# Relative values in an attention kernel: table parts side by side, both probability parts in one matmul, mask on GpSimd

## The chip, the core and the metric

The kernel runs on one core of a Trainium2 chip. The metric is the device time of one execution in microseconds; the median of the runs shown counts. TensorE is PE in the rows of the profile (its weight loads PEld), VectorE is DVE, ScalarE is ACT, GpSimd is POOL, and SyncE, which issues the DMAs, is SP. On-chip memory is SBUF; PSUM is the memory that matmuls write to.

## The reference

Two batches of 2048 tokens with 256 features go through a layer norm, then through attention with relative positions and through a mixture of experts (8 experts, top 2), which are added to the input. The attention has 16 heads of 16 features each, so there are 32 (batch, head) pairs of 2048 x 2048 scores:

```python
rel_pos = jnp.arange(L)[None, :] - jnp.arange(L)[:, None] + (MAX_LEN - 1)
rel_k = relative_k[rel_pos]          # indices outside the 511 rows wrap or clamp
rel_v = relative_v[rel_pos]
scores = jnp.einsum('bhld,bhrd->bhlr', Q, K) * scale
scores = scores + jnp.einsum('bhld,lrd->bhlr', Q, rel_k)
attn = jax.nn.softmax(scores, axis=-1)
out = jnp.einsum('bhlr,bhrd->bhld', attn, V)
out = out + jnp.einsum('bhlr,lrd->bhld', attn, rel_v)
```

The change is in the last line, the relative values: for query row l and key row r the row `rel_v[l, r]` depends on r - l alone. Far from the diagonal it is a constant row, which the kernel adds to V. Near the diagonal (9 key blocks of 128 around each query block of 128, offsets -6 to 2) it is worked out from a table.

## The kernel before

The program has three stages, one after the other: `project` (layer norm, projections, router), the attention stage, and `mix` (experts and output). The change touches a little of the first and the middle one.

**Units and steps.** A unit is one query block of 128 rows (16 per head, `NB`) of one of the 32 heads, so 512 units. The attention stage is a software pipeline over k = 0, 1, 2, ...: in step k each engine works at several units that lie some steps apart (`LAG_S`, `LAG_A`, `LAG_X`, `LAG_PV` are 3, 4, 5 and 6). The order of instructions on each engine is the order of the code in its `step` function; there is no planner. Eight units are a half head (`HALF_C`).

**What a step does.** PE multiplies queries and keys into the score banks (L918), turns the scores so that keys lie on partitions (L952 and L960), and multiplies probabilities and values (L984). DVE reads each score bank once for the maximum (L1146 and L1150, `search_bank`). ACT takes the exponentials of four banks into `pt_full` (L1077). Each of the four becomes a high part in 16 bits (a cast: `high_part`, two on DVE at L1170, two on ACT at L1085) and a low part, the difference to the full number (a subtraction: `low_part`, three on GpSimd at L850, the fourth on DVE at L1178). High parts are cast first, since the low parts read them; GpSimd's first low part of a unit waits for DVE's first cast of it. On DVE a step runs: sums and masks of the relative values if there are any, searches of banks 0 and 2, the fourth low part of the unit before, the two casts, searches of banks 1 and 3, the maximum.

**Relative values.** The parts of the probabilities near the diagonal stay in `pt_near[half]` (part, unit of the half head, offset, query). For a half head `rel_values` (L1011) runs through 16 groups a of 8 neighbouring queries (`SHIFTS` is 8). The stationary operand is a window of 128 columns of the table, in which partition p holds the rows of `rel_v` shifted by p; its 128 columns are 8 shifts of 16 features. The moving operand is 64 columns, 8 units by 8 queries, so every query meets all 8 shifts although only one is its own. Table and probabilities are each split in a high and a low part, and three matmuls are made per offset: high table with high probabilities, high table with low ones, low table with high ones. This makes 16 x 9 x 3 = 432 matmuls for a half head, 54 in a step. Eight groups fill the one PSUM bank `r_ps`; DVE then multiplies the bank by the 0/1 mask of the right shifts into `rel_out` in SBUF (`mask_values`, L1203, twice in a half head), and PE waits for this before it fills the bank again. Afterwards PE turns `rel_out` (`pick_values`, L1026) and DVE sums over the shifts (`sum_values`, L1211). GpSimd adds this to the values' part and scales it (`output`, L861 and L864).

**GpSimd's other work.** In four steps of each head (k % 16 from 7 to 10) it also prepares the values of the next head (`v_part`, L835 to L839), two instructions a step.

## Time and profile before

| | |
|---|---|
| Median of 3 runs | 3461.26 us (3460.48 to 3466.33) |
| Span of the profiled execution | 3463.7 us, 165,894 instructions |
| PE busy over the span | 3194.2 us (92%) |
| DVE | 2813.3 us (81%) |
| ACT | 2634.6 us (76%) |
| POOL | 2262.5 us (65%) |
| Granted TensorE clock, mean | 0.953 of full speed |

For the profiled execution the page gives its span, from the first to the last instruction, and no time of its own beside it; the span is 2.4 us above the median of the runs. The attention stage takes about 2700 us of it. Busy time of an engine is the union of its instructions; a matmul's entry includes its latency, so that PE can count as busy while it could take more work. Neighbouring entries on DVE and POOL overlap a little for the same reason.

### The profile page before, as it was taken

To read this page: it belongs to the slowest core of one execution; us is meant where nothing else is said; L and a number is where in the kernel's file an instruction comes from. 1 tells how busy PE (TensorE), PEld (TensorE's weight loads), DVE (VectorE), ACT (ScalarE), POOL (GpSimd) and SP (SyncE) were. 2 spreads that over 40 slices of the span, in tenths; PEclk is the share of its full clock that TensorE was granted. 3 is DMA by queue.
4 is the path that set the end of the run, shared out by engine and by line. 5 is a ranking of instruction groups with operands and counts; after the bars stand their busy time and mean duration, and the time that the engine had idled before them with its cause. 6 is when DMAs were issued, how large, how long until landed. Compare 5 with 4: busy or idle time off the path is not lost. (4 is left out here: it accounts for less than half of the span.)

```text
span 3463.7 us, 165894 instructions
## 1 busy us (share of the span) xinstructions
PE 3194.2 (92%) x64918; PEld 2524.8 (73%) x64918; DVE 2813.3 (81%) x7853; ACT 2634.6 (76%) x5852; POOL 2262.5 (65%) x2526
## 2 busy tenths in 40 slices
PE   7589999999999999999999999999999996999990
PEld 4357777777777777777777777777777785579980
DVE  6479999999999999999999999999999986534443
ACT  3288888888888888888888888888888893234440
POOL 0167777777777777777777777777777774700006
PEclk9779999999999999999999999999999997589995
DMA  7776666666666666666666666666666664712224
GB/s 212 228 230 216 221 220 221 221 221 224 218 221 224 221 223 224 222 218 224 221 223 224 223 217 221 224 224 221 224 218 222 222 217 161 239 51 69 62 62 145
DMA packets 356374, 701.28 MB, mean 202 GB/s; under 512 B 59545, under 2 KB 168706, under 8 KB 355346
## 3 DMA queue, kind: packets, MB, share of 16 engines
q1 hardware_dynamic: 349458, 673.92, 60.3%
q0 software_dynamic: 6144, 16.79, 1.5%
q8 instruction: 518, 8.49, 1.1%
q14 instruction: 254, 2.08, 0.2%
HBM read 343.02 MB, written 347.46 MB: 199 GB/s over the span
## 5 line engine op out<-in xcount | busy, mean ns | idle before, releaser
L850 POOL TENSOR_TENSOR pt_near<-pt_full,pt_near 128x512 f16<-128x512 f32 (+3 forms) x1984 | 1857.7, 965 | 583.8 <-DVE pt_near L1170 583.8
L1077 ACT ACTIVATE pt_full<-pb,exp_bias 128x512 f32<-128x512 f32 x2048 | 1313.5, 688 | 305.7 <-PE pb L960 183.9
L1011 PEld LDWEIGHTS pb<-pt_near,table_high 128*128 128x128 f16 x18432 | 794.6, 97 | 145.1 <-issue 106.4
L1011 PE MATMUL pb<-pt_near,table_high 128*128 128x64 f16 (+6 forms) x18432 | 884.8, 187 | 15.7 <-DVE rel_out L1203 14.6
L1150 DVE TENSOR_REDUCE part_max<-pb 128x1 f32<-128x512 f32 (+3 forms) x1376 | 771.2, 574 | 131.0 <-PE pb L918 130.0
L1011 PE MATMUL pb<-pt_near,table_low 128*128 128x64 f16 (+6 forms) x9216 | 851.4, 187 | 0.0
L1011 PEld LDWEIGHTS pb<-pt_near,table_low 128*128 128x128 f16 x9216 | 772.7, 97 | 0.0
L1146 DVE CUSTOM_DVE_ANT_0 near_sum<-pb,skewed 128x512 bf16<-128x512 f32 (+3 forms) x1216 | 675.6, 571 | 109.4 <-PE pb L918 85.0
L952 PE MATMUL pb<-ident,skewed 128*128 128x128 f32 x3840 | 621.6, 285 | 20.5 <-ACT q_max L1101 19.2
L1170 DVE CAST pt_near<-pt_full 128x512 f16<-128x512 f32 (+3 forms) x1280 | 532.3, 466 | 0.3 <-PE pb L984 0.3
L984 PE MATMUL pb<-v_head,pt_near 128*128 128x33 f16 x13440 | 507.2, 178 | 9.1 <-POOL pt_near L850 5.5
L984 PEld LDWEIGHTS pb<-v_head,pt_near 128*128 128x128 f16 x13440 | 431.6, 96 | 48.3 <-POOL pt_near L850 31.0
L1069 ACT COPY rel<-pb 128x384 f32<-128x384 f32 x1024 | 437.6, 486 | 37.2 <-PE pb L901 32.4
L952 PEld LDWEIGHTS pb<-ident,skewed 128*128 128x128 f32 x3840 | 409.0, 141 | 49.0 <-ACT q_max L1101 32.2
L1085 ACT CAST pt_near<-pt_full 128x512 f16<-128x512 f32 (+3 forms) x896 | 426.5, 527 | 0.0
L918 PE MATMUL pb<-k_stack,q_stack 48*128 48x512 f16 (+3 forms) x2592 | 402.0, 336 | 24.3 <-DVE part_max L1146 18.0
L960 PE MATMUL pb<-q_max,k_stack 50*128 50x128 f16 x8192 | 409.8, 220 | 15.6 <-ACT pt_full L1077 13.6
L960 PEld LDWEIGHTS pb<-q_max,k_stack 50*128 50x128 f16 x8192 | 232.5, 95 | 183.9 <-issue 137.9
L1479 POOL DMA_INDIRECT stage<-y_slots_scratch,slot x64 | 60.6, 947 | 366.4 <-DMA y_slots_scratch<-y_group 347.2
L1178 DVE TENSOR_TENSOR pt_far<-pt_full,pt_far 128x512 f16<-128x512 f32 (+3 forms) x416 | 293.8, 706 | 0.0
L1085 ACT CAST pt_far<-pt_full 128x512 f16<-128x512 f32 (+3 forms) x416 | 247.0, 594 | 0.0
L901 PE MATMUL pb<-rk_stack,q_stack 48*128 48x384 f16 x1024 | 179.9, 326 | 39.2 <-DMA q_stack<-planes_scratch 30.5
(182 smaller groups left out, 4063.3 us busy)
## 6 DMA issues: line engine op xcount, KB each, us to landing
skewed<-rel_scratch SPq DMA_DIRECT2D x256, 576.0 KB, 5.3
rel_scratch<-rel SPq DMA_DIRECT2D x416, 319.5 KB, 3.4
rel_scratch<-rel SPq DMA_DIRECT2D x320, 320.0 KB, 2.8
skewed<-rel_scratch SPq DMA_DIRECT2D x64, 512.0 KB, 4.6
skewed<-rel_scratch SPq DMA_DIRECT2D x64, 448.0 KB, 4.3
k_stack<-planes_scratch SPq DMA_DIRECT2D x192, 96.0 KB, 4.7
planes_scratch<-planes SPq DMA_DIRECT2D x64, 256.0 KB, 2.3
rel_scratch<-rel SPq DMA_DIRECT2D x64, 256.0 KB, 2.7
```

The source lines that it names most:

```text
L850: ins = nc.gpsimd.tensor_tensor(pt_piece(c, 1, a, z, near), pt_full[e][:, (a - 4 * g) * P:(z - 4 * g) * P], pt_piece(c, 0, a, z, near), AL ...
L918: ins = nc.tensor.matmul(ps[:, a - bank * CH:z - bank * CH], q_stack[b][tile_rows(tile), c * P:(c + 1) * P], k_stack[b][tile_rows(tile), k ...
L952: nc.tensor.matmul(x_ps[e % 2][:, (blk - 4 * g) * P:(blk - 4 * g + 1) * P], skewed[u % 4][:, col:col + P], keep["ident"][:, :], is_transpo ...
L960: ins = nc.tensor.matmul(x_ps[e % 2][:, i * P:(i + 1) * P], k_stack[b][tile_rows(tile, STACK + 2), kind_of(c, blk), col:col + P], q_max[u ...
L984: ins = nc.tensor.matmul(o_ps[:, i * VW:(i + 1) * VW], src[:, cols], rhs, start=(blk == 0 and part == 0), stop=(blk == NB - 1 and part == 1))
L1011: ins = nc.tensor.matmul(acc[:, c0:c1, :], keep[table][:, w:w + P], pt_near[half][:, part, c0:c1, d - M_LO, a * SHIFTS:(a + 1) * SHIFTS], ...
L1069: nc.scalar.copy(rel[k % 2][:, n * half:(n + 1) * half], bank_of("rel", k, n)[:, 0:half]).then_inc(s_ge, 1)
L1077: nc.scalar.activation(pt_full[e][:, :], x_ps[e % 2][:, :], ACT.Exp, bias=exp_bias[:, 0:1]).then_inc(s_exp, 1)
L1085: ins = nc.scalar.copy(pt_piece(c, 0, a, z, near), pt_full[e][:, (a - 4 * g) * P:(z - 4 * g) * P])
L1146: ins = nc.vector.tensor_tensor_reduce(out=near_sum[:, col:col + z - a], in0=src, in1=skewed[k % 4][:, col:col + z - a], scale=1.0, scalar ...
L1150: ins = nc.vector.tensor_reduce(best, src, axis=AX.X, op=ALU.max)
L1170: ins = nc.vector.tensor_copy(pt_piece(c, 0, a, z, near), pt_full[e][:, (a - 4 * g) * P:(z - 4 * g) * P])
```

## The change

The table's high and low part now lie side by side, 16 features of the one and 16 of the other, so that a window of 128 columns holds 4 shifts of both. `SHIFTS` falls to 4 and the groups of queries rise to 32. The moving operand holds both parts of the probabilities, 2 x 8 units x 4 queries = 64 columns, in runs of 4 neighbouring elements where there were 8. One matmul then makes all four products (the low table with the low probabilities was not made before). A half head takes 32 x 9 = 288 matmuls, 36 in a step.

The two halves of the bank (high and low probabilities) must be added. DVE does this as it reads the bank: a reduction over pairs into a new SBUF buffer `rel_raw` (`read_values`). The bank now fills four times in a half head, so there are four such reads where there were two masks. The mask moves to GpSimd, which reads `rel_raw` and writes `rel_out` (`mask_values`, two in a half head, each 16 groups x 8 units x 4 queries, 512 elements per partition). The transposes come one step later (`LAG_SEL`), and so do the sums on DVE and the output on GpSimd. In the first stage the table is written to memory and read back in two DMAs instead of four, with the same bytes.

```diff
-SHIFTS = P // DK
+PLANES = 2
+SHIFTS = P // (PLANES * DK)
+COPIES = PLANES * SHIFTS
...
-LAG_SEL = LAG_RV + HALF_C
+LAG_SEL = LAG_RV + HALF_C + 1
...
+FILLS = 4
+FILL_A = SHIFT_GROUPS // FILLS
...
+            def mask_values(it, h, part):
...
+                pool.wait_ge(s_rle, FILLS * h + (part + 1) * FILLS // 2)
+                if part == 0 and h:
+                    pool.wait_ge(s_sel, PICK_BANKS * h)
+                half_a = SHIFT_GROUPS // 2
+                rows = slice(part * half_a, (part + 1) * half_a)
+                dst = rel_out[:, :, rows, :].rearrange("p c a b -> p a c b")
+                src = rel_raw[:, rows, :].rearrange("p a (c b) -> p a c b", c=HALF_C)
+                mask = keep["shift_mask"][:, :].rearrange("p (x y b) -> p x y b", x=1, y=1)
+                nc.gpsimd.tensor_tensor(dst, src, mask.to_broadcast([P, half_a, HALF_C, SHIFTS]), ALU.mult).then_inc(s_rlm, 1)
...
                 if exists(it, u):
                     for e in range(E - 1):
                         low_part(it, u, e)
+                for part in range(2):
+                    h, j = half_at(k, LAG_RV + (part + 1) * (HALF_C // 2))
+                    if j == 0 and h >= 0 and exists(it, h * HALF_C):
+                        mask_values(it, h, part)
...
-                a = 2 * j + quarter // 2
-                ds = range(M_LO, M_HI + 1)
-                order = (0, 1, -1, -2, 2, -3, -4, -5, -6)
-                order = order[:5] if quarter % 2 == 0 else order[5:]
...
-                    w = table_window(d, a) * DK
-                    for n, (table, part) in enumerate((("table_high", 0), ("table_high", 1), ("table_low", 0))):
-                        ins = nc.tensor.matmul(
-                            acc[:, c0:c1, :], keep[table][:, w:w + P],
-                            pt_near[half][:, part, c0:c1, d - M_LO, a * SHIFTS:(a + 1) * SHIFTS],
...
+                    w = table_window(d, a) * PLANES * DK
+                    ins = nc.tensor.matmul(
+                        acc[:, :, c0:c1, :], keep["table"][:, w:w + P],
+                        pt_near[half][:, :, c0:c1, d - M_LO, a * SHIFTS:(a + 1) * SHIFTS],
...
+            def read_values(it, h, n):
...
+                dve.wait_ge(s_rl, FILLS * h + n + 1)
+                if n % 2 == 0 and h:
+                    dve.wait_ge(s_rlm, 2 * (h - 1) + n // 2 + 1)
+                src = r_ps[:, :].rearrange("p (a q m) -> p a m q", a=FILL_A, q=PLANES)
+                nc.vector.tensor_reduce(rel_raw[:, n * FILL_A:(n + 1) * FILL_A, :], src, axis=AX.X,
+                                        op=ALU.add).then_inc(s_rle, 1)
...
-                h, j = half_at(k, LAG_RV + 4)
-                if j == 0 and h >= 0 and exists(it, h * HALF_C):
-                    mask_values(it, h, 0)
-                h, j = half_at(k, LAG_RV + 8)
-                if j == 0 and h >= 0 and exists(it, h * HALF_C):
-                    mask_values(it, h, 1)
+                for n in range(FILLS):
+                    h, j = half_at(k, LAG_RV + (n + 1) * (HALF_C // FILLS))
+                    if j == 0 and h >= 0 and exists(it, h * HALF_C):
+                        read_values(it, h, n)
```

How the order moves is seen at three places. The first is GpSimd, in the four steps of a head that also hold value work; this is the order before, in which L850 are low parts, L861 and L864 the output, and L835 to L839 the value work:

```order
75 L850 TENSOR_TENSOR pt_near<-pt_full,pt_near 128x384
76 L861 TENSOR_TENSOR out<-rel_sum,o_sum 128x128
77 L864 TENSOR_TENSOR out<-out,inv_sum 128x128
78 L837 CAST v_head<-v_in 128x16x16
79 L839 TENSOR_TENSOR v_head<-v_in,v_head 128x16x16
80 L850 TENSOR_TENSOR pt_near<-pt_full,pt_near 128x512 x2
81 L850 TENSOR_TENSOR pt_near<-pt_full,pt_near 128x256 x2
82 L835 TENSOR_TENSOR v_full<-v_in,rv_lo 128x256
83 L837 CAST v_head<-v_full 128x16x16
```

The same place of the changed kernel, where L856 are the low parts, L872 is the mask, and L880 and L883 are the output:

```order
78 L856 TENSOR_TENSOR pt_near<-pt_full,pt_near 128x384
79 L843 CAST v_head<-v_in 128x16x16
80 L845 TENSOR_TENSOR v_head<-v_in,v_head 128x16x16
81 L856 TENSOR_TENSOR pt_near<-pt_full,pt_near 128x512 x2
82 L856 TENSOR_TENSOR pt_near<-pt_full,pt_near 128x256 x2
83 L880 TENSOR_TENSOR out<-rel_sum,o_sum 128x128
84 L883 TENSOR_TENSOR out<-out,inv_sum 128x128
85 L841 TENSOR_TENSOR v_full<-v_in,rv_lo 128x256
86 L843 CAST v_head<-v_full 128x16x16
87 L856 TENSOR_TENSOR pt_near<-pt_full,pt_near 128x512 x2
88 L856 TENSOR_TENSOR pt_near<-pt_full,pt_near 128x384
89 L856 TENSOR_TENSOR pt_near<-pt_full,pt_near 128x128
90 L872 TENSOR_TENSOR rel_out<-rel_raw,shift_mask 128x16x8x4
```

The output stands one step later, and a mask follows the low parts of a step, ahead of the value work; it stands so in four steps of each head (k % 16 of 1, 5, 9 and 13), three of which have no value work.

The second is DVE at the step in which the sums stand. Before, the two sums (L1211) and the read of the values' bank (L1189, L1190) follow the maximum (L1160, L1162) and precede the next searches:

```order
347 L1160 TENSOR_REDUCE neg_max<-part_max 128x1
348 L1162 TENSOR_REDUCE max_parts<-part_max 128x2
349 L1211 TENSOR_REDUCE rel_sum<-pb 128x64 x2
350 L1189 RECIPROCAL inv_sum<-pb 128x8
351 L1190 TENSOR_REDUCE o_sum<-pb 128x128
352 L1146 ISA near_sum,part_max<-pb,skewed 128x512
```

In the changed kernel a read of the relative values' bank (L1220) stands behind the sums (L1229):

```order
361 L1180 TENSOR_REDUCE neg_max<-part_max 128x1
362 L1182 TENSOR_REDUCE max_parts<-part_max 128x2
363 L1229 TENSOR_REDUCE rel_sum<-pb 128x64 x2
364 L1220 TENSOR_REDUCE rel_raw<-pb 128x256
365 L1166 ISA near_sum,part_max<-pb,skewed 128x512
```

The read of the values' bank has stayed in its step, and is now one step ahead of the sums; the other three reads of a half head stand two, four and six steps behind, each alone at the start of its step.

The third is PE, one group a of the relative values. Before, it is 27 matmuls, of which the first 9 are:

```order
220 L1011 MATMUL pb<-pt_near,table_high 128x64 x2
221 L1011 MATMUL pb<-pt_near,table_low 128x64
222 L1011 MATMUL pb<-pt_near,table_high 128x64 x2
223 L1011 MATMUL pb<-pt_near,table_low 128x64
224 L1011 MATMUL pb<-pt_near,table_high 128x56 x2
225 L1011 MATMUL pb<-pt_near,table_low 128x56
```

In the changed kernel it is 9:

```order
216 L1031 MATMUL pb<-pt_near,table_pairs 128x64 x2
217 L1031 MATMUL pb<-pt_near,table_pairs 128x2x28
218 L1031 MATMUL pb<-pt_near,table_pairs 128x2x24
219 L1031 MATMUL pb<-pt_near,table_pairs 128x64
220 L1031 MATMUL pb<-pt_near,table_pairs 128x2x20
221 L1031 MATMUL pb<-pt_near,table_pairs 128x2x16
222 L1031 MATMUL pb<-pt_near,table_pairs 128x2x12
223 L1031 MATMUL pb<-pt_near,table_pairs 128x2x8
```

A step holds four such groups where it held two of the old ones; the numbers of columns are the same.

## Rows read from the trace of the kernel before

**Rows 1.** The view by cores: span and mean granted clock.

```profile
core 0: 3463.7 us, clock 0.953
```

**Rows 2.** Busy time by stretch (from:to, length, each engine with its instructions).

```profile
1000.00:2000.00 1000.00, 969.18 (x22698) 771.60 (x22692) 911.55 (x2631) 888.31 (x2009) 780.45 (x879) 1.00 0.68 221
```

**Rows 3.** ACT's groups by form, 1000 to 2000 us: count | busy, mean ns.

```profile
L1091 ACT ACTIVATE max_parts<-max_parts,neg_max 128x2 bf16<-128x2 bf16 x190 | 57.2, 301 | 0.0
```

**Rows 4.** The waits, 1000 to 2000 us: total us, times, longest.

```profile
POOL pt_near L850 <- DVE pt_near L1170: 210.9, 154, 2.7
ACT pt_full L1077 <- PE pb L960: 63.8, 118, 1.4
...
DVE part_max L1150 <- PE pb L918: 47.1, 72, 1.5
...
DVE near_sum L1146 <- PE pb L918: 30.2, 48, 1.0
```

**Rows 5.** The timeline of POOL, 1440 to 1530 us: start, length, [idle before].

```profile
1458.22 3.44 POOL L850 TENSOR_TENSOR pt_near<-pt_full,pt_near 128x512 f16<-128x512 f32 x3 [2.36 <-DVE pt_near L1170]
...
1501.75 3.59 POOL L850 TENSOR_TENSOR pt_near<-pt_full,pt_near 128x384 f16<-128x384 f32 x4 [2.14 <-DVE pt_near L1170]
1506.61 3.45 POOL L850 TENSOR_TENSOR pt_near<-pt_full,pt_near 128x512 f16<-128x512 f32 x3 [1.27 <-DVE pt_near L1170]
...
1511.90 3.60 POOL L850 TENSOR_TENSOR pt_near<-pt_full,pt_near 128x512 f16<-128x512 f32 x4 [0.90 <-DVE pt_near L1170]
```

**Rows 6.** The timeline of DVE in a step without extra work.

```profile
1504.23 0.69 DVE L1150 TENSOR_REDUCE part_max<-pb 128x1 f32<-128x512 f32 x1 [0.66 <-PE pb L918]
...
1505.44 0.69 DVE L1178 TENSOR_TENSOR pt_far<-pt_full,pt_far 128x512 f16<-128x512 f32 x1
1506.05 0.76 DVE L1170 CAST pt_near<-pt_full 128x512 f16<-128x512 f32 x2
```

**Rows 7.** The timeline of POOL in a step with value work.

```profile
1482.59 1.16 POOL L850 TENSOR_TENSOR pt_near<-pt_full,pt_near 128x512 f16<-128x512 f32 x1
1483.69 0.88 POOL L837 CAST v_head<-v_full 128x256 f16<-128x256 f32 x1
1484.72 0.68 POOL L839 TENSOR_TENSOR v_head<-v_full,v_head 128x256 f16<-128x256 f32 x1
1485.35 1.16 POOL L850 TENSOR_TENSOR pt_near<-pt_full,pt_near 128x512 f16<-128x512 f32 x1
```

**Rows 8.** The timeline of DVE in the same step.

```profile
1483.09 1.20 DVE L1178 TENSOR_TENSOR pt_far<-pt_full,pt_far 128x512 f16<-128x512 f32 x1
1484.22 2.50 DVE L1170 CAST pt_near<-pt_full 128x512 f16<-128x512 f32 x3
```

**Rows 9.** DVE's groups by form, 1000 to 2000 us.

```profile
L1150 DVE TENSOR_REDUCE part_max<-pb 128x1 f32<-128x512 f32 x310 | 210.4, 685 | 35.2 <-PE pb L918 34.9
...
L1203 DVE TENSOR_TENSOR rel_out<-pb,shift_mask 128x512 f32<-128x512 f32 x48 | 32.7, 681 | 0.0
...
L1211 DVE TENSOR_REDUCE rel_sum<-pb 128x64 f32<-128x512 f32 x46 | 29.6, 685 | 3.0 <-PE pb L1026 2.7
```

**Rows 10.** The timeline of PE: one group of relative values, and what follows it.

```profile
1504.18 0.23 PE L1011 MATMUL pb<-pt_near,table_high 128*128 128x64 f16 x2
...
1504.91 0.55 PE L984 MATMUL pb<-v_head,pt_near 128*128 128x33 f16 x16
```

**Rows 11.** POOL's groups by form, 1000 to 2000 us.

```profile
L850 POOL TENSOR_TENSOR pt_near<-pt_full,pt_near 128x512 f16<-128x512 f32 x405 | 467.0, 1172 | 135.0 <-DVE pt_near L1170 135.0
...
L835 POOL TENSOR_TENSOR v_full<-v_in,rv_lo 128x256 f32<-128x256 f32 x12 | 10.9, 908 | 0.0
```

**Rows 12.** DVE's timeline at the start of the step that holds the sums.

```profile
1454.24 1.29 DVE L1211 TENSOR_REDUCE rel_sum<-pb 128x64 f32<-128x512 f32 x2 [0.23 <-PE pb L1026]
1455.44 0.20 DVE L1189 RECIPROCAL inv_sum<-pb 128x8 f32<-128x8 f32 x1
1455.56 0.37 DVE L1190 TENSOR_REDUCE o_sum<-pb 128x128 f32<-128x256 f32 x1
1455.85 0.68 DVE L1146 CUSTOM_DVE_ANT_0 near_sum<-pb,skewed 128x512 bf16<-128x512 f32 x1
```

**Rows 13.** Groups of the attention stage's last stretch, 2881 to 2900.5 us.

```profile
L1011 PE MATMUL pb<-pt_near,table_high 128*128 128x64 f16 (+2 forms) x288 | 13.7, 196 | 0.8 <-DVE rel_out L1203 0.8
...
L1203 DVE TENSOR_TENSOR rel_out<-pb,shift_mask 128x512 f32<-128x512 f32 x2 | 1.4, 692 | 9.7 <-PE pb L1011 9.7
```

66 lines of the change are left out of this document (30 added, 36 removed).

## The prediction, on record before the result

> **What bounds the kernel now.** I began with the span [rows 1] and took a thousand microseconds from the middle of the attention stage [rows 2]. There PE is busy 969 us, DVE 912, ACT 888 and POOL 780, at the full granted clock. ACT runs one instruction of L1091 per step, 190 of them [rows 3], so a step takes 5.26 us and a head of 16 steps 84.2 us; 32 heads are 2695 us. Read this way PE is the bound, and the waits seem to say so too: DVE waits for PE's scores and ACT for its turned scores [rows 4].
>
> The longest wait in the table says something else. POOL waits 210.9 us for DVE's cast L1170, 154 times, 1.37 us each [rows 4], while it is only 78% busy. So I laid the timelines of POOL and DVE side by side. In a plain step POOL ends its three low parts at 1501.75 + 3.59 = 1505.34 and starts the next at 1506.61 [rows 5]. In that gap DVE runs its own low part L1178 (1505.44) and then the cast that POOL waits for (1506.05) [rows 6]. DVE's low part starts when POOL stops, and that is no accident, as a step with value work shows: L1178 started at 1483.09 takes 1.20 us where the plain step's takes 0.69, and ends 0.54 us after POOL's 1482.59 + 1.16 = 1483.75. POOL's next, begun at 1483.69, takes 0.88 for 256 elements. Three casts that start at 1484.22 take 2.50 us, where two take 0.76 in the plain step [rows 6, 7, 8]. DVE's instructions that read PSUM are not stretched like this: L1150, L1203 and L1211 have means of 685, 681 and 685 ns at 512 elements, whatever POOL does [rows 9]. So POOL's instructions and DVE's instructions with SBUF sources alone (L1178, L1170) take turns, whole instructions at a time, and the two together are one resource.
>
> How full is it? A plain gap must hold the low part up to the cast (0.61 us), the cast (0.42) and the start of POOL (0.14), 1.17 us [rows 5, 6]. There are 154 / 11.9 = 13 gaps in a head (the value steps have none), 17.8 us, of which 13 x 1.17 = 15.2 are needed. Only 2.6 us of 84.2 are slack. Of it 2 x 1.19 lie at the steps with the sums, where DVE is busy with PSUM reads before its low part (gap 2.36) [rows 5, 12]. So PE and the pair POOL/DVE are both nearly full.
>
> The Trainium skill (SBUF — State Buffer, "Who interferes with whom") gives the rule: GpSimd and VectorE share one pair of ports, held by one of them for a whole instruction; VectorE needs it for casts in its two-port modes and for two SBUF inputs, but not with a PSUM source. It agrees with rows 7 to 9. It speaks against this change: by it a mask on GpSimd counts in full against DVE's casts, while the DVE reads of PSUM cost nothing there, the same sum as below.
>
> **The change, part by part.**
>
> *Fewer matmuls.* 27 matmuls run from 1504.18 to 1504.91, 27 ns each [rows 10]. A half head has 144 fewer: 3.9 us, 7.8 a head. PE's share goes from 0.969 x 84.2 = 81.6 us to 73.8. This holds if a matmul whose moving operand comes in runs of 4 elements costs what one with runs of 8 does. No row shows it. Below, it can gain nothing (columns and weight loads are the same); above I allow twice the time (twice as many runs): 288 x 54 ns = 15.6 against 11.7 us. I take the same 27 ns, because windows of few columns and of many run at nearly the same pace within the group.
>
> *Four reads instead of two masks on DVE.* A reduction of 512 PSUM elements is 685 ns, 0.61 from start to start [rows 6, 9]. Eight reads less four masks a head: +2.4 us. DVE goes from 76.8 (0.912 x 84.2) to 79.2 us a head. They use none of the shared resource, and in most steps they lie beside POOL's low parts, 3.45 us long, in place of the 0.66 that DVE waits there for PE [rows 5, 6]. At the step of the sums, one read (0.61) replaces the reciprocal and the read of the values' bank (1455.44 to 1455.85, 0.41) [rows 12]: +0.2 us, twice a head, which I leave inside the rounding. Nothing cheaper than zero is possible; uncovered in full they would cost 2.4 us a head.
>
> *Mask on GpSimd.* No row shows this instruction. The nearest of 512 elements is L850, 1.17 us, 3 of them in 3.45 [rows 5, 11]: 1.15. From above, L835, also with a broadcast operand and a 32-bit result, takes 0.91 for 256 elements [rows 11], so 1.8. I take 1.15, for the count of elements and inputs is the same. Four masks a head are 4.6 us of the shared resource. Queued behind a mask are the value work and the next step's low parts, which wait for DVE's cast anyway; that cast and DVE's low part now stand behind the mask, and DVE is in order, so searches, PE's banks and ACT follow. The other side cannot hide it, for there are 2.6 us of slack, and at the sums' steps there is no mask.
>
> *What PE gives back.* When PE is no longer late, the plain gaps shrink toward 1.17. At least 2.6 - 2.4 = 0.2 and at most 2.6 us a head can be recovered. I take the middle, 1.4. ACT's 0.888 x 84.2 = 74.8 us does not bind.
>
> *One step later.* The output (0.9 us of POOL) moves from one step to the next with its length unchanged: 0. The pick, the new wait of PE, is for a mask that was issued a step before: 0. If the mask is late, PE waits and so does what stands behind it, the next turned scores, but PE has 0.6 us a step in hand.
>
> *Ends of the stage.* In the last 20 us the relative values stand alone on PE [rows 13]: 144 x 30 ns = 4.3 less, two more hand-overs of the bank (0.69 + 0.3 each) and a mask: 4.3 - 2.0 - 1.2 = 1 us gained. The table's DMAs carry the same bytes: 0.
>
> **Sum.** Per head 4.6 - 1.4 = +3.2 us, over 32 heads +102, less 1: +101. Against the profiled span 3463.7 this is 3565; the median of the runs is 2.4 lower, so 3562 us. The likeliest case has its own range: all slack recovered gives +2.0 a head (3524), none +4.6 (3607).
>
> **Rivals.**
>
> *PE is the bound, and GpSimd has room.* For it: 969 of 1000 us busy, DVE and ACT waiting for it, POOL idle for 22%. If the masks fit into POOL's gaps without delaying the cast, the head is set by DVE, 79.2 us at the share that PE now has (0.97): 81.7, or -2.5 a head, -80 us: 3380. Half of this, with masks half hidden: -40, 3421. It decides as soon as a mask delays DVE's low part by less than 0.35 us (1.4 of recovered slack over four masks). Against it are the stretched casts. 20%.
>
> *No change to be seen.* As the likeliest, but a mask costs just what is recovered: POOL's two output instructions in the step before 1511.90 shortened the gap behind them to 0.90, so part of such work is absorbed [rows 5]. 3461. 8%.
>
> *The mask is dear.* At 1.8 us: 7.2 - 1.4 = 5.8 a head, +186: 3646. 5%.
>
> *Short runs slow PE.* At twice the time per matmul PE needs 81.6 + 7.8 = 89.4 us a head, +5.2 at least, +166: 3625. The Trainium skill (Advanced Engine Details and Errata, "Memory Cachelines") has lines of 16 bytes in SBUF and wants at least two hits on each; runs of 4 have four hits on 8 bytes, so by that rule there is no penalty. 5%.
>
> *The likeliest:* 62%.
>
> **The numbers.** Slower by over 0.2% (about what can be told from no change here): 62 + 5 + 5 = 72%, same 8%, faster 20%. The range goes from 3420, the half-hidden case, to 3625, the slow-run bound; it leaves out the full gain, about 12%, and most of the dear mask.
>
> **What would show it.** Right: casts L1190 and low parts L1198 on DVE with longer means than now, the mask at 1.1 to 1.3 us, PE's busy share down to about 85%, hardly any wait of DVE for PE, a step of about 5.46 us, and steps with a mask 0.7 to 1.2 us longer than plain ones. Wrong: masks that run inside POOL's gaps while DVE's low part is elsewhere, a step under 5.26, or relative-value matmuls at another pace than 27 ns.

## The result and the profile after

| | before | after |
|---|---|---|
| median of 4 runs each, us | 3462.98 (3460.48 to 3466.33) | 3530.91 (3528.64 to 3533.72) |
| ratio with 95% interval | | 1.0194 [1.0179, 1.0208] |
| span of the profiled execution, us | 3463.7 | 3529.7 |
| mean granted clock | 0.953 | 0.949 |

The changed kernel is slower by 1.9%, 68 us. I had forecast slower, by 101 us: 3562. First the page's engine totals, then the middle of the attention stage (length, then PE, PEld, DVE, ACT, POOL, PEclk, DMA share, GB/s), which answers to [rows 2].

```profile
PE 3053.4 (87%) x55702; PEld 2305.4 (65%) x55702; DVE 2971.6 (84%) x7981; ACT 2659.6 (75%) x5852; POOL 2421.2 (69%) x2654
```

```profile
1000.00:2000.00 1000.00, 895.43 (x18813) 674.02 (x18813) 947.16 (x2621) 874.34 (x1958) 814.63 (x901) 0.99 0.66 215
```

PE fell from 969 to 895 us of a thousand, DVE rose from 912 to 947 and POOL from 780 to 815. No engine is now as near to full as PE was, and the kernel is slower, so no single full engine explains the loss. The groups by form of the same stretch (count | busy, mean ns | idle before):

```profile
L856 POOL TENSOR_TENSOR pt_near<-pt_full,pt_near 128x512 f16<-128x512 f32 x393 | 459.4, 1187 | 122.2 <-DVE pt_near L1190 122.2
...
L1190 DVE CAST pt_near<-pt_full 128x512 f16<-128x512 f32 x276 | 148.4, 572 | 0.0
...
L1198 DVE TENSOR_TENSOR pt_far<-pt_full,pt_far 128x512 f16<-128x512 f32 x114 | 98.3, 862 | 0.0
...
L1220 DVE TENSOR_REDUCE rel_raw<-pb 128x256 f32<-128x512 f32 x93 | 63.4, 681 | 0.2 <-issue 0.2
L856 POOL TENSOR_TENSOR pt_near<-pt_full,pt_near 128x256 f16<-128x256 f32 x94 | 61.3, 673 | 15.2 <-DVE pt_near L1190 15.2
L872 POOL TENSOR_TENSOR rel_out<-rel_raw,shift_mask 128x512 f32<-128x512 f32 x46 | 59.0, 1283 | 0.0
L1111 ACT ACTIVATE max_parts<-max_parts,neg_max 128x2 bf16<-128x2 bf16 x185 | 55.1, 298 | 0.0
```

ACT's row x185 says how many steps there were, 1000 / 185 = 5.41 us each; counted over 28 heads (the table below) a step is 5.40 us and a head 86.4, where it was 84.3. The mask, L872, takes 1.28 us on average. Of the same view of the kernel before, two rows are worth setting beside these:

```profile
L1170 DVE CAST pt_near<-pt_full 128x512 f16<-128x512 f32 x287 | 138.7, 518 | 0.0
L1178 DVE TENSOR_TENSOR pt_far<-pt_full,pt_far 128x512 f16<-128x512 f32 x118 | 92.4, 783 | 0.0
```

The cast went from 518 to 572 ns and DVE's low part from 783 to 862, while its reads of PSUM stand at 681 as before. The waits of the stretch (total us, times, longest) answer to [rows 4]:

```profile
POOL pt_near L856 <- DVE pt_near L1190: 177.3, 143, 2.4
ACT pt_full L1097 <- POOL pt_near L856: 52.1, 94, 1.3
ACT pt_full L1097 <- PE pb L983: 50.8, 61, 1.4
...
DVE part_max L1170 <- PE pb L941: 29.8, 58, 1.6
...
PE pb L1031 <- DVE rel_raw L1220: 17.1, 46, 0.5
...
DVE near_sum L1166 <- PE pb L941: 14.8, 25, 0.9
```

DVE's two waits for PE's scores are 45 us instead of 77, so PE did come earlier; POOL waits less for DVE because the masks fill some of its gaps. One such gap, on POOL's timeline and then on DVE's:

```profile
1529.64 3.81 POOL L856 TENSOR_TENSOR pt_near<-pt_full,pt_near 128x256 f16<-128x256 f32 x5 [2.14 <-DVE pt_near L1190]
1533.41 1.48 POOL L872 TENSOR_TENSOR rel_out<-rel_raw,shift_mask 128x512 f32<-128x512 f32 x1
1535.39 3.58 POOL L856 TENSOR_TENSOR pt_near<-pt_full,pt_near 128x384 f16<-128x384 f32 x4 [0.50 <-DVE pt_near L1190]
```

```profile
1532.51 0.68 DVE L1166 CUSTOM_DVE_ANT_0 near_sum<-pb,skewed 128x512 bf16<-128x512 f32 x1
1533.12 0.08 DVE L1166 DVE_READ_ACCUMULATOR2_ANT part_max<- 128x1 f32 x1
1533.12 0.88 DVE L1198 TENSOR_TENSOR pt_far<-pt_full,pt_far 128x512 f16<-128x512 f32 x1
1533.92 1.66 DVE L1190 CAST pt_near<-pt_full 128x384 f16<-128x384 f32 x3
```

The mask goes in at 1533.41, right where POOL used to stand idle, and DVE's three casts behind it take 1.66 us (without a mask the same three take 0.82, as the next section shows). The low parts of the step behind begin 5.75 us after those of the step before (1535.39 less 1529.64).

### The profile page after: what moved, and what is told of

Its sections match the earlier page's. It is cut to its first block and busy times, and to the rows that moved or that the text cites. A ratio compares the mean times of both kernels' runs of the same rounds, so it can differ in the third digit from the quotient of the medians.

```text
span 3529.7 us, 147842 instructions
## 1 busy us (share of the span) xinstructions
PE 3053.4 (87%) x55702; PEld 2305.4 (65%) x55702; DVE 2971.6 (84%) x7981; ACT 2659.6 (75%) x5852; POOL 2421.2 (69%) x2654
## 5 line engine op out<-in xcount | busy, mean ns | idle before, releaser
L856 POOL TENSOR_TENSOR pt_near<-pt_full,pt_near 128x512 f16<-128x512 f32 (+3 forms) x1984 | 1861.6, 967 | 494.6 <-DVE pt_near L1190 494.5
L1097 ACT ACTIVATE pt_full<-pb,exp_bias 128x512 f32<-128x512 f32 x2048 | 1340.3, 690 | 347.2 <-POOL pt_near L856 143.1
L975 PE MATMUL pb<-ident,skewed 128*128 128x128 f32 x3840 | 633.2, 287 | 95.7 <-ACT q_max L1121 82.7
L1031 PE MATMUL pb<-pt_near,table_pairs 128*128 128x64 f16 (+6 forms) x18432 | 664.9, 187 | 52.0 <-DVE rel_raw L1220 50.5
L1031 PEld LDWEIGHTS pb<-pt_near,table_pairs 128*128 128x128 f16 x18432 | 574.6, 96 | 181.7 <-DVE rel_raw L1220 98.6
L1007 PE MATMUL pb<-v_head,pt_near 128*128 128x33 f16 x13440 | 529.5, 178 | 67.3 <-POOL pt_near L856 54.4
L1190 DVE CAST pt_near<-pt_full 128x512 f16<-128x512 f32 (+3 forms) x1280 | 549.0, 478 | 0.4 <-PE pb L1007 0.4
L1105 ACT CAST pt_near<-pt_full 128x512 f16<-128x512 f32 (+3 forms) x896 | 427.3, 528 | 0.0
L941 PE MATMUL pb<-k_stack,q_stack 48*128 48x512 f16 (+3 forms) x2592 | 400.4, 337 | 9.1 <-DVE part_max L1166 3.2
L1198 DVE TENSOR_TENSOR pt_far<-pt_full,pt_far 128x512 f16<-128x512 f32 (+3 forms) x416 | 347.7, 836 | 0.0
L1105 ACT CAST pt_far<-pt_full 128x512 f16<-128x512 f32 (+3 forms) x416 | 248.1, 596 | 0.0
L924 PE MATMUL pb<-rk_stack,q_stack 48*128 48x384 f16 x1024 | 190.6, 328 | 52.4 <-DMA q_stack<-planes_scratch 30.4
L1698 DVE SCALAR_TENSOR_TENSOR hidden<-pc,up_bias,silu 128x256 f32<-128x256 f32 x156 | 68.5, 480 | 145.8 <-PE pc L1794 145.6
L1220 DVE TENSOR_REDUCE rel_raw<-pb 128x256 f32<-128x512 f32 x256 | 174.4, 681 | 8.2 <-PE pb L1031 8.0
```

The lines of the kernel that those rows point to most:

```text
L856: ins = nc.gpsimd.tensor_tensor(pt_piece(c, 1, a, z, near), pt_full[e][:, (a - 4 * g) * P:(z - 4 * g) * P], pt_piece(c, 0, a, z, near), AL ...
L941: ins = nc.tensor.matmul(ps[:, a - bank * CH:z - bank * CH], q_stack[b][tile_rows(tile), c * P:(c + 1) * P], k_stack[b][tile_rows(tile), k ...
L975: nc.tensor.matmul(x_ps[e % 2][:, (blk - 4 * g) * P:(blk - 4 * g + 1) * P], skewed[u % 4][:, col:col + P], keep["ident"][:, :], is_transpo ...
L1007: ins = nc.tensor.matmul(o_ps[:, i * VW:(i + 1) * VW], src[:, cols], rhs, start=(blk == 0 and part == 0), stop=(blk == NB - 1 and part == 1))
L1031: ins = nc.tensor.matmul(acc[:, :, c0:c1, :], keep["table"][:, w:w + P], pt_near[half][:, :, c0:c1, d - M_LO, a * SHIFTS:(a + 1) * SHIFTS] ...
L1097: nc.scalar.activation(pt_full[e][:, :], x_ps[e % 2][:, :], ACT.Exp, bias=exp_bias[:, 0:1]).then_inc(s_exp, 1)
```

## The experiments

To see where the time sits, I also took each trace apart by the loop's steps. DVE searches a maximum (`neg_max`) once in each step; the table gives the mean time from one to the next over 28 heads, by the number of the later step in its head (k modulo 16). Masks stand at the end of POOL's steps 1, 5, 9 and 13, so they act on the intervals 2, 6, 10 to 12 and 14. The sums stand in 6 and 14 before, in 7 and 15 after. The columns are experiments that follow below.

```
k     before  after  a_no_mask  a_one_under  a_mask_under  b_fewer_   b_fewer_  b_pool_work  a_two_masks
                                _sums        _sums         matmuls    pool_work
2      5.13   5.54     4.69        5.53          4.69        5.04       5.67       5.65        6.39
3      5.01   4.61     4.85        4.62          4.85        4.88       4.61       4.61        4.75
6      5.96   5.47     4.63        4.62          4.63        5.62       5.62       5.96        6.32
7      4.56   5.81     5.81        5.82          6.48        4.48       4.47       4.56        6.00
11     6.89   7.26     7.66        7.16          7.67        6.89       6.06       6.03        8.55
12     4.17   5.36     4.37        5.30          4.46        4.26       5.38       5.39        6.28
14     5.84   5.29     4.61        4.58          4.72        5.77       5.78       5.77        6.12
15     4.90   5.89     5.89        5.89          6.62        4.65       4.65       4.91        5.89
head  84.32  86.40    83.55       84.70         84.37       82.40      83.75      84.97       91.51
```

Three more quantities are sums over 26 heads in the middle of the stage, divided by 26. Stretch is the time by which DVE's casts and low parts last longer than the same form does undisturbed (at 512 elements 419 and 684 ns): 5.2 us a head before, 8.1 after. DVE's wait for PE is the part of its idle time that ended when PE's scores came (L918, now L941): 6.5 before, 3.9 after. PE's busy time is 81.7 before and 77.3 after.

### The change without its mask: a_no_mask

```diff
-                    pe.wait_ge(s_rlm, 2 * h + 2)
+                    pe.wait_ge(s_rle, FILLS * (h + 1))
...
-                nc.vector.tensor_reduce(rel_raw[:, n * FILL_A:(n + 1) * FILL_A, :], src, axis=AX.X,
-                                        op=ALU.add).then_inc(s_rle, 1)
...
+                dst = rel_out[:, :, n * FILL_A:(n + 1) * FILL_A, :].rearrange("p c a b -> p a c b")
+                nc.vector.tensor_reduce(dst, src, axis=AX.X, op=ALU.add).then_inc(s_rle, 1)
```

The call of `mask_values` on GpSimd goes too, DVE's `read_values` writes to `rel_out` directly, and PE's pick waits for it. The multiplication by the mask is left out of this kernel.

> The changed kernel without the mask: the four reads write straight into rel_out, GpSimd does no relative-value work, and the shifts that the mask would clear stay in the sums (so this leaves out the masking). Theory, shared ports: the four masks of a head (1.28 us each in the changed kernel) stood in the chain of GpSimd and VectorE, so a head falls from 86.4 us to about 82 (86.4 - 4.6), the time to about 3390; VectorE's casts and low parts get shorter again. Rival, hand-overs: the loss came from VectorE's four reads and TensorE's four waits for the bank, GpSimd had room; then the time stays within 10 us of the changed kernel's 3531.

Measured: 3437.30 us, ratio 0.9918 [0.9901, 0.9934], between the 3390 of my theory and the 3531 of the rival. Of the changed kernel's 3530.9 us the mask is 94 us, 2.9 a head. Everything else in the change together is a gain of 28 us. The same stretch and the two groups of DVE:

```profile
1000.00:2000.00 1000.00, 916.69 (x19457) 691.88 (x19457) 950.86 (x2705) 900.24 (x2024) 789.00 (x887) 1.00 0.69 223
```

```profile
L1186 DVE CAST pt_near<-pt_full 128x512 f16<-128x512 f32 x286 | 138.1, 517 | 0.0
...
L1194 DVE TENSOR_TENSOR pt_far<-pt_full,pt_far 128x512 f16<-128x512 f32 x120 | 91.6, 764 | 0.0
```

Cast and low part are back at 517 and 764 ns, so what lengthened them was the mask. The step shown above, on POOL's timeline of this kernel and with the three casts of DVE:

```profile
1483.79 3.69 POOL L856 TENSOR_TENSOR pt_near<-pt_full,pt_near 128x256 f16<-128x256 f32 x5 [1.13 <-DVE pt_near L1186]
1488.85 3.59 POOL L856 TENSOR_TENSOR pt_near<-pt_full,pt_near 128x384 f16<-128x384 f32 x4 [1.38 <-DVE pt_near L1186]
```

```profile
1488.22 0.82 DVE L1186 CAST pt_near<-pt_full 128x384 f16<-128x384 f32 x3
```

It lasts 5.06 us from start to start, with the mask 5.75: 0.69 more for an instruction of 1.48. In the table the four masks cost 0.71 (k = 2 to 4), 0.84 (6), 0.59 (11 and 12) and 0.68 (14), the same picture. The stretch is 5.6 us a head without the mask and 8.1 with it: 2.5 more, though the masks are 4 x 1.28 = 5.1 us long. I laid each mask beside DVE's instructions (means over the same 26 heads, us):

```
mask behind the    length  beside DVE's low    beside DVE's    costs in the
low parts of step          part and casts      PSUM reads      table
1                  1.36    1.36                0.00            0.71
5                  1.47    1.46                0.01            0.84
9                  1.22    0.32                0.90            0.59
13                 1.06    0.79                0.27            0.68
```

A mask that nothing disturbs takes 1.04 us (`a_mask_under_sums` below), so about 0.9 of the 5.1 us is the masks' own waiting. Another 1.2 lies beside DVE's PSUM reads, nearly all of it at one place, step 9. The masks of steps 1 and 5 have no such cover, and still cost somewhat less than 1.04; what spares that remainder no run shows. Step 9 is a step with value work, and there the cost takes another way. Even without the mask POOL is idle for only 0.14 us of interval 10, and ACT's wait for POOL's low parts in interval 11 rises from 0.72 us to 1.76 with the mask, by a whole mask's length. Much of this mask lies beside PSUM reads and it is paid for all the same, in GpSimd's own queue.

### The kernel before with work of the mask's size on GpSimd: b_pool_work

```diff
+            def extra_work(it, h, part):
+                pool.wait_ge(s_spare, 2 * h + part + 1)
+                src = spare_in[:, :, :].rearrange("p a (c b) -> p a c b", c=HALF_C)
+                dst = spare_out[:, :, :, :].rearrange("p c a b -> p a c b")
+                mask = keep["shift_mask"][:, 0:4].rearrange("p (x y b) -> p x y b", x=1, y=1)
+                nc.gpsimd.tensor_tensor(dst, src, mask.to_broadcast([P, 16, HALF_C, 4]), ALU.mult).then_inc(s_spare, 1)
```

GpSimd calls it where the change has its masks. The computation is unchanged, and nobody reads `spare_out`.

> The kernel before with nothing changed but one more GpSimd multiplication (the mask's shape, on spare buffers in SBUF) at the four places of a head where the changed kernel has its masks. Theory, shared ports: GpSimd is idle 22% of the time and yet the work is not free; a head grows from 84.3 us by 2.5 to 4.6 (the slack of 2.6 is partly used), the time to 3540 to 3605. Rival, TensorE is the bound and GpSimd has room: 3463, within 8 us.

Measured: 3486.35 us, 1.0061 [1.0045, 1.0078], +21 us or 0.65 a head. The added group by form:

```profile
L864 POOL TENSOR_TENSOR spare_out<-spare_in,shift_mask 128x512 f32<-128x512 f32 x48 | 51.9, 1082 | 0.0
```

I had expected 3540 to 3605, and the rival 3463; it came out between them, nearer the rival. An instruction of the same shape, 1.08 us here, costs less than a quarter of what the mask costs in the changed kernel. The table says where the rest went. At 6 and 14 it costs nothing (5.96 and 5.96; 5.84 and 5.77), since there DVE has the sums before its low part, and the whole instruction lies beside PSUM reads. At 2 it costs 0.52, and 0.40 comes back in step 3. Most of what is left lies at the value steps: interval 10 (not in the table) rises by 0.17, and 11 and 12 together by 0.36. The stretch grows by 1.4 us, and DVE's wait for PE falls by 0.9 (6.5 to 5.6): where PE is late, DVE has time to lose. DVE's casts of 512 elements are at 560 ns and its low parts at 845, nearly as long as in the changed kernel.

### Fewer matmuls alone: b_fewer_matmuls

```diff
-                    for n, (table, part) in enumerate((("table_high", 0), ("table_high", 1), ("table_low", 0))):
+                    for n, (table, part) in enumerate((("table_high", 0), ("table_high", 1))):
...
```

The kernel before with 288 relative-value matmuls a half head, the changed kernel's number; the product of the low table with the high probabilities is left out.

> The kernel before without the product of the table's low part and the high probabilities (that part of the computation is left out): 288 matmuls a half head in the old shape, as many as the changed kernel has, all else as before. Theory, shared ports: TensorE's 7.8 us a head are given back only as far as the pair GpSimd/VectorE has slack, 0.2 to 2.6 us a head, I say 1.4: 3418, at the least 3380. Rival, TensorE is the bound: up to the next engine (VectorE, 76.8 us of work), 4 us or more a head, 3330 or below.

Measured: 3406.67 us (3400.22 to 3412.37), 0.9838 [0.9821, 0.9854], -58 us (3418 expected), 1.9 a head by the table. The table's execution is the fastest of the four, 6 us under their median, so 1.9 is a little high; 5 us more are gained behind the last search (589.5 us from there to the end, 594.7 before). PE is busy 5.5 us less a head (81.7 to 76.2), and DVE's wait for PE goes from 6.5 to 5.0. What the head recovers is a third of what PE was spared. POOL's gaps closed by as much, from 17.9 us a head to 15.9, close to the 15.2 that the prediction worked out as needed; this is the row of its wait, beside 210.9 in [rows 4]:

```profile
POOL pt_near L850 <- DVE pt_near L1170: 194.1, 158, 2.6
```

### Both: b_fewer_pool_work

The two edits above in one kernel.

> The kernel before with both edits that were made singly: the low table's product left out, and the mask-sized GpSimd work added. Theory A, cover: of the four, two stand ahead of the steps with the sums and are hidden there in both kernels; the other two are paid once TensorE no longer gives the time back, 0.6 to 1.0 us each, 1.2 to 2.0 a head: 3407 + 40 to 65 = 3447 to 3472. Rival, no interaction (the two edits add up, -58 + 21): 3428.

Measured: 3445.54 us, 0.9942 [0.9925, 0.9959], just under the 3447 to 3472 expected and well over the rival's 3428. On top of fewer matmuls the GpSimd work costs 39 us (1.35 a head by the table) and not 21. So about 18 us of its price is there only because PE was relieved (the two differences are from different groups of runs, each against its neighbour). The steps 6 and 14 are still free (5.62 and 5.62; 5.77 and 5.78), and step 2 rises by 0.63 to 5.67.

### Two more reads alone: b_fewer_reads

```diff
+            def extra_read(it, h, n):
+                dve.wait_ge(s_spare, 2 * h + n + 1)
+                nc.vector.tensor_reduce(spare_out[:, :, :], spare_in[:, :, :, :].rearrange("p a q m -> p a m q"), axis=AX.X,
+                                        op=ALU.add).then_inc(s_spare, 1)
```

DVE calls it with the lags LAG_RV + 2 and LAG_RV + 6, on top of `b_fewer_matmuls`, whose product is left out here too.

> The kernel before without the low table's product (left out, as in the run with fewer matmuls, 3407), and with two more reductions of 512 elements on VectorE in each half head, at the two steps where the changed kernel has a read and the kernel before has no mask; they read a spare SBUF buffer (one source), so no bank is held longer. It prices VectorE's reads alone. The changed kernel without its mask stands 30 us above the run with fewer matmuls. Theory B, VectorE is in order and its time counts: four reductions of 0.61 us a head, half of them covered, +1.2 us a head: 3430 to 3445. Rival, the reads lie beside GpSimd's low parts as predicted and the 30 us come from the hand-overs of the bank: 3407, within 8 us.

Measured: 3416.24 us, 0.9857 [0.9840, 0.9873]. Against `b_fewer_matmuls` that is +10 us by the medians and +7 by the ratios, and the profiled executions give 0.57 us a head, +18, which is too much by what was said of that kernel's fast execution. The two ratio intervals overlap, though every time here lies above every time there (3413.71 at the least against 3412.37 at the most). So the price is small and its size is not well known; my 3430 to 3445 was too high, and the rival's 3407 within 8 is missed by 1 us. The read itself, by form:

```profile
L1211 DVE TENSOR_REDUCE spare_out<-spare_in 128x256 f32<-128x512 f32 x49 | 33.6, 685 | 0.0
```

Four of 0.68 us in a head are 2.7 us of DVE, and DVE's wait for PE falls by 1.8 (5.0 to 3.2). Two thirds of a read are taken out of that wait. From here to `a_no_mask` (3437.3) some 20 us are left, for which the sums that now share a step with a read, twice as many hand-overs of the bank, the matmuls' new operand and the pick a step later are there to blame. PE's own wait for DVE's reads of the bank hardly differs, 1.05 us a head there and 0.95 here. No run splits the rest.

### The mask twice: a_two_masks

```diff
                 nc.gpsimd.tensor_tensor(dst, src, mask.to_broadcast([P, half_a, HALF_C, SHIFTS]), ALU.mult).then_inc(s_rlm, 1)
...
+                spare = spare_out[:, :, :, :].rearrange("p c a b -> p a c b")
+                nc.gpsimd.tensor_tensor(spare, src, mask.to_broadcast([P, half_a, HALF_C, SHIFTS]), ALU.mult).then_inc(s_spare, 1)
```

> The changed kernel with each mask made twice on GpSimd, the second time into a spare buffer. In the first four runs the mask cost 94 us in the changed kernel (3437 without it) but the same GpSimd work only 21 in the kernel before. Theory A, cover: of 5.1 us of masks a head 2.9 were paid, because part of each lay beside VectorE's PSUM reads; a second mask right behind finds no cover left and is paid in full, 4 x 1.15 = 4.6 us a head: 3531 + 147 = 3678. Rival, a fixed share: as the first, 2.9 a head: 3625.

Measured: 3687.82 us, 1.0640 [1.0622, 1.0657], 157 us over the changed kernel. By the table that is 5.1 us a head for four instructions of 1.21 us, 4.9 (expected: 3678, paid in full). The first masks cost 2.9 us a head, the second ones on average their full length. By place they differ: 1.0 us in the intervals 2 to 4 and 1.0 in 6 and 7, 0.8 in 14, but 2.2 in 11 and 12. That dear one, at step 9, takes no time beside DVE's low part and casts (0.75 of its 1.04 us lie beside PSUM reads, the rest beside short maxima or nothing), and ACT's wait for POOL's low parts in interval 11 goes from 1.8 us to 3.2 by it. Only 1.9 of it shows as stretch (8.1 to 10.0). DVE's wait for PE grows by 2.0 (3.9 to 5.9), ACT's for POOL's low parts from 4.6 to 6.8 and PE's for them from 1.8 to 3.4: at the value steps POOL is late in its own queue, and a mask that takes nothing from DVE's casts delays the low parts behind it instead. The granted clock of the stretch is 0.96 here (0.99 in the changed kernel), which was not separated.

```profile
L874 POOL TENSOR_TENSOR rel_out<-rel_raw,shift_mask 128x512 f32<-128x512 f32 x44 | 55.7, 1266 | 0.0
L878 POOL TENSOR_TENSOR spare_out<-rel_raw,shift_mask 128x512 f32<-128x512 f32 x44 | 53.4, 1214 | 0.0
```

The wait of ACT for POOL, beside 52.1 in the changed kernel:

```profile
ACT pt_full L1103 <- POOL pt_near L858: 77.0, 97, 3.2
```

### The mask on ScalarE: a_mask_act

```diff
+                for r in range(SHIFTS):
+                    rows, b = slice(PLANES * DK * r, PLANES * DK * (r + 1)), SHIFTS - 1 - r
+                    ins = nc.scalar.copy(dst[rows, b, :, :], src[rows, b, :, :])
+                ins.then_inc(s_rlm, 1)
```

ACT does this behind its high parts. On each group of 32 partitions the mask keeps one shift and sets the others to zero; four copies of the kept quarter into a `rel_out` that was zeroed once do the same, away from GpSimd.

> The changed kernel with the mask made by ScalarE instead of GpSimd: four copies a mask, each of 32 partitions and of the one shift that these keep (128 elements), into a buffer whose other places are zero. The whole computation is made. Theory A: ScalarE does not take turns with VectorE; it has 8 us of idle time a head and gets 3.2 more of work; near the kernel without a mask, 3437 to 3460, at or under the kernel before. Rival: ScalarE, at 75.5 of 86.4 us, becomes late for TensorE and the time stays at 3490 or above.

Measured: 3573.75 us, 1.0313 [1.0296, 1.0330], slower than the changed kernel by 43 us; I had expected 3437 to 3460. By form:

```profile
L1132 ACT COPY rel_out<-rel_raw 32x128 f32<-32x128 f32 x180 | 76.6, 426 | 1.6
```

A copy of 128 elements on 32 partitions takes 426 ns, so a mask is 1.7 us of ACT, and this runs in one piece ahead of the next exponentials. PE waits for ACT's exponentials 4.2 us a head, 0.5 in the changed kernel, and POOL for DVE's cast 19.8 us a head, where it was 15.1:

```profile
POOL pt_near L856 <- DVE pt_near L1204: 226.4, 160, 3.9
...
PE pb L971 <- ACT pt_full L1093: 25.4, 34, 1.2
...
PE pb L979 <- ACT pt_full L1093: 21.5, 22, 1.6
```

ACT is 81 of 87.6 us busy, 92%. The mask left the pair GpSimd/VectorE, and the delay came in ahead of it, at the exponentials that its casts read. Where the mask stands in ACT's step was not varied. Two things stay open: DVE's casts of 512 elements still take 556 ns with no mask on GpSimd, and the granted clock of the stretch is 0.97 (0.99 in the changed kernel).

### The mask inside the reads: a_quadrants

```diff
-                nc.vector.tensor_reduce(rel_raw[:, n * FILL_A:(n + 1) * FILL_A, :], src, axis=AX.X,
-                                        op=ALU.add).then_inc(s_rle, 1)
...
+                for r in range(SHIFTS):
+                    rows, b = slice(PLANES * DK * r, PLANES * DK * (r + 1)), SHIFTS - 1 - r
+                    ins = nc.vector.tensor_reduce(dst[rows, b, :, :], src[rows, b, :, :, :], axis=AX.X, op=ALU.add)
+                ins.then_inc(s_rle, 1)
```

Here DVE sums only the kept quarter, in four reductions of 32 partitions, into a zeroed `rel_out`: the full computation without any mask.

> The changed kernel with another mask: the mask keeps one shift per 32 partitions, so VectorE reads each bank with four reductions of 32 partitions (128 elements each) that write only the kept shift into rel_out, whose other places are zero from the start. The whole computation is made, and GpSimd has no mask. Theory, shared ports: no mask in the chain, -4.6 us a head, but 4 x 0.2 = 0.8 us a read in place of 0.61, +1.6 us of VectorE a head beside GpSimd's work: about 83 us a head, 3420, faster than both kernels. Rival, VectorE or the hand-overs are the bound: the longer reads make it slower than the changed kernel, 3580.

Measured: 3513.30 us, 1.0140 [1.0123, 1.0157], faster than the changed kernel by 18 us and 76 over the one without a mask. I had expected 3420, with reductions of 0.2 us. By form, and then the waits:

```profile
L1219 DVE TENSOR_REDUCE rel_out<-pb 32x64 f32<-32x128 f32 x373 | 106.8, 286 | 3.8
```

```profile
PEld pb L1027 <- DVE rel_out L1219: 69.0, 70, 1.3
PE pb L1027 <- DVE rel_out L1219: 49.0, 70, 1.0
```

Four reductions of 286 ns are 1.14 us for 0.68, so the single bank of relative values is held 0.46 us longer at every hand-over, eight times a head. PE's waits for it, 17 us of a thousand in the changed kernel, are 49. The stretched casts are gone (520 ns, low parts 819), but another wait took their place.

### One mask under the sums: a_one_under_sums

```diff
-LAG_SEL = LAG_RV + HALF_C + 1
+LAG_SEL = LAG_RV + 2 * HALF_C + 1
...
-                    h, j = half_at(k, LAG_RV + (part + 1) * (HALF_C // 2))
+                    h, j = half_at(k, LAG_RV + (part + 1) * (HALF_C // 2) + part)
```

The second mask of a half head is issued one step later, between the low parts of steps 6 and 7 (14 and 15), where DVE then has the sums. So that the pick finds it done, pick, sums and output come a half head later, with one more buffer each for `rel_out`, `o_sum` and `inv_sum` and one fewer for `rel_sum`. The computation and the number of instructions are those of the changed kernel.

> The changed kernel with the second mask of each half head one step later, so that it stands ahead of the step in which VectorE makes the sums and a read, 1.8 us without SBUF sources only; the pick, the sums and the output come 8 steps later, with a second rel_out and a third o_sum, so that the heavy step stays where it was. The first mask stays. Theory A, cover: the steps behind the second masks were 0.84 and 0.68 us longer than without a mask, and this goes: -1.5 us a head, 3531 - 48 = 3483. Rival, the place does not matter since GpSimd and VectorE have no time left between them: 3531, within 8 us.

Measured: 3477.10 us, 1.0032 [1.0020, 1.0045], 54 us less than the changed kernel (3483 expected). In the table the intervals 6 and 14 fall to what they are without a mask (4.62, 4.58), and 7 and 15, where the mask now lies, do not move (5.82, 5.89). A GpSimd instruction that costs 0.76 us in one place costs nothing one step later, where all of its 1.04 us lies beside DVE's PSUM reads.

### Both masks under the sums: a_mask_under_sums

```diff
-                    h, j = half_at(k, LAG_RV + (part + 1) * (HALF_C // 2))
+                    h, j = half_at(k, LAG_RV + HALF_C + 1)
```

As above, with a third half buffer for `rel_raw`, since the first half waits longer for its mask.

> As the run with one mask under the sums (3477), but with both masks of a half head, one behind the other, ahead of the step with the sums and a read (and a second buffer for the first half of the raw sums). It measures how much a heavy step covers: there GpSimd had a gap of 2.36 us of which 1.17 are needed, so 1.2 us are free. Theory A, cover: of two masks of 1.2 us the second is paid, +1.2 us a half head, while the first masks' old places give back 0.6 each: 84.7 + 2.4 - 1.2 = 85.9 us a head, 3515. Rival, a heavy step hides them both: 83.6 us a head, 3440, under the kernel before.

Measured: 3461.93 us over 10 runs, 0.9995 [0.9985, 1.0004]: level with the kernel before, 69 us better than the changed kernel. I had thought the second mask would be paid in full there, as in `a_two_masks`, and come to 3515; the rival, both masks free, was 3440. POOL's timeline of such a step, and DVE's:

```profile
1498.40 3.59 POOL L856 TENSOR_TENSOR pt_near<-pt_full,pt_near 128x384 f16<-128x384 f32 x4 [1.10 <-DVE pt_near L1190]
1501.95 2.04 POOL L872 TENSOR_TENSOR rel_out<-rel_raw,shift_mask 128x512 f32<-128x512 f32 x2
1505.02 3.45 POOL L856 TENSOR_TENSOR pt_near<-pt_full,pt_near 128x512 f16<-128x512 f32 x3 [1.03 <-DVE pt_near L1190]
```

```profile
1500.13 1.28 DVE L1231 TENSOR_REDUCE rel_sum<-pb 128x64 f32<-128x512 f32 x2
1501.33 0.68 DVE L1222 TENSOR_REDUCE rel_raw<-pb 128x256 f32<-128x512 f32 x1
1501.92 0.68 DVE L1170 TENSOR_REDUCE part_max<-pb 128x1 f32<-128x512 f32 x1
1502.52 0.68 DVE L1166 CUSTOM_DVE_ANT_0 near_sum<-pb,skewed 128x512 bf16<-128x512 f32 x1
1503.13 0.09 DVE L1166 DVE_READ_ACCUMULATOR2_ANT part_max<- 128x1 f32 x1
1503.13 1.41 DVE L1198 TENSOR_TENSOR pt_far<-pt_full,pt_far 128x512 f16<-128x512 f32 x1
1504.46 0.75 DVE L1190 CAST pt_near<-pt_full 128x512 f16<-128x512 f32 x2
```

POOL ends its low parts at 1501.99, and DVE reads PSUM until 1503.2. The first mask fits in there. The second keeps DVE's low part waiting, 1.41 us where 0.69 is its length, and the casts behind it take their undisturbed 0.75. So two masks cost 0.7 us together (intervals 7 and 15: 5.81 to 6.48 and 5.89 to 6.62). Both masks take 1.04 us each here, unstretched, where they take 1.28 in the changed kernel. Against `a_one_under_sums` the intervals 2 and 12 get 0.84 us shorter each, but 7 and 15 get 0.66 and 0.73 longer and 11 another 0.51. The interval behind 15 (k = 0, not in the table) gets 0.48 shorter, and the head is 0.33 us shorter in all.

## Why the prediction was right, and what was off in it

**The bound: right.** The mask on GpSimd lengthens DVE's casts and low parts and nothing else there: 518 to 572 and 783 to 862 ns with it, 517 and 764 without it, DVE's reads of 512 PSUM elements at 680 to 685 in all of them. The two swaps by one factor (`a_no_mask`, `b_pool_work`) and the move of the same instruction by one step (`a_one_under_sums`) show it. The Trainium skill (SBUF — State Buffer, "Who interferes with whom") has this rule, a shared port pair held for whole instructions, which PSUM reads leave alone; these numbers agree with it.

**The step that was mis-sized: "The other side cannot hide it, for there are 2.6 us of slack, and at the sums' steps there is no mask."** I paid all four masks in full, 4.6 us a head. They cost 2.9: 94 us for 147. The size of a mask was not the error (listed with 1.28 us, alone 1.04, for my 1.15). The error was that I priced a mask without looking at what DVE does beside it. Of the 5.1 us that the four are listed with, about 0.9 is their own waiting and 1.2 lies beside DVE's reads of PSUM, which leaves 3.0, close to the 2.9 paid; 2.5 of it is seen as stretch of DVE's casts and low parts. Place by place this is less tidy: most of the cover is at step 9, where the mask is paid for in GpSimd's own queue, and why the masks of steps 1 and 5 cost 0.71 and 0.84 and not 1.04 is open. That a place can hide the work is shown by moving it: the same work costs 0.65 us a head in the kernel before, and one mask under the sums costs nothing. That the hiding is bounded is shown by the second mask there, 0.7 us, and by `a_two_masks`, where the second ones cost their full length. My own remark on the gap of 2.36 at the sums [rows 5] had the cover in it; I used it as slack of the head and not as a place.

**What PE gives back: under-sized, within its bounds.** 1.4 us a head taken from 0.2 to 2.6; `b_fewer_matmuls` measures 1.9 (58 us, not 45, of which 5 lie behind the last search). My forecast of the profile was too strong on PE: DVE, said to wait hardly at all for it, still waits 3.9 us a head, and PE is 89.5% busy, not 85. Its busy time falls by 5.5 us a head in `b_fewer_matmuls`, where 288 matmuls at 27 ns are 7.8; the matmuls' ends are modelled, and that difference stays open. (The bound of the slow-run rival, 3625, comes to 3627 by its own terms, which moves nothing.)

**The reads: not free.** Taken as nothing, they are some 7 to 10 us in `b_fewer_reads` (its interval overlaps that of its neighbour), and with the sums, the hand-overs and the later pick the rest of the change besides matmuls and mask costs 31 us (3406.7 to 3437.3), about 1 us a head. I had looked for what hides them in each step's wait for PE; it does hide two thirds of a read, but the same waits were what the fewer matmuls were to recover, and I spent them twice.

**Short runs: right.** From start to start matmuls of 64 columns take 29.0 ns on average before and 29.6 after.

**The sum.** Predicted: -45 for matmuls, 0 for reads, +147 for masks, -1 for the end: +101. Measured: -58, +31, +94: +67, against 68 seen. These three are steps of one chain of kernels, so they have to add up, and in another order each could come out differently, as the GpSimd work did (21 us or 39). The mask's error of 53 is the largest; the 31 of the reads hid part of it, and that the total is off by 31 us and not more is to this extent luck. The ends of the stage gave nothing (594.7 us from the last search to the end of the span in both kernels). The likeliest case's own range, 3524 to 3607, holds 3531 near its lower end, and steps are 5.40 us where I said 5.46. Of the signs I had named, longer casts and low parts and a mask of 1.1 to 1.3 us came out. A step with a mask is 0.59 to 0.84 us longer, where I said 0.7 to 1.2, and the two signs on PE did not come out.

**The rival "PE is the bound, and GpSimd has room"** fails: a mask delays the head by 0.71 us on average, twice the 0.35 at which it was to decide. It is half right in the kernel before, where 21 us is what the added work costs.

**What would be faster.** No version with the full computation beats the kernel before beyond its interval; `a_mask_under_sums` is level with it. The 58 us of the matmuls are all spent again, some 30 on reads and hand-overs and some 25 on masks that still stretch a low part. Only kernels that leave part of the computation out (`b_fewer_matmuls`, `b_fewer_reads`, `a_no_mask`) are below 3440.

## What to carry to other kernels

When GpSimd and VectorE are both busy with SBUF data, a GpSimd instruction has no price of its own, only one for its place. Here 1.04 us of it cost nothing beside VectorE's reads of PSUM where GpSimd had a gap, 0.7 to 0.8 us beside VectorE's low part and casts, and 0.6 us, or 2.2 for a second one, in a step in which GpSimd itself had no gap left, though most of it lay beside those reads. So two things must be seen: lay the two timelines side by side, find where GpSimd falls idle before VectorE is through with PSUM, and put the work there. Moving one of two masks by one step was worth 54 us here. And count a wait once: time that one term of the sum recovers cannot also hide another.

## What the hardware showed that I had not expected

A copy on ScalarE of 32 partitions x 128 elements took 426 ns, where its casts of 128 x 128 take 273 from PSUM (L1121) and 315 from SBUF (L1105): a quarter of the partitions was no cheaper. The copy also has a strided source and result, which was not separated. The GpSimd mask, 512 elements with a strided result, takes 1.04 us undisturbed and 1.28 on average when it alternates with DVE, up to 1.5. VectorE's reductions of 32 partitions x 128 elements take 286 ns, as its 128 x 128 ones do (284). In `a_two_masks` the mean granted clock of the program was 0.925, and 0.96 from 1000 to 2000 us, where the changed kernel has 0.949 and 0.99; what that cost was not separated, so its 5.1 us a head may hold a little of it.
